# Attention inside a two-layer block: projections in the transposes' banks, a score bank per head, and the causal mask added by VectorE

## The reference

```
h = x_norm                                   # (2, 1024, 256)
q = (h @ wq) -> 32 heads of 64;  k, v = (h @ wk), (h @ wv) -> 8 heads of 64
scores = q @ k.T / sqrt(64)                  # each KV head serves 4 query heads
scores = where(causal, scores, min)
attn = softmax(scores);  out = (attn @ v) @ wo
```

## Time and profile before

| | us |
|---|---|
| median of 3 runs | 2073.08 |
| range of the runs | 2064.65 to 2074.55 |
| the profiled execution | 2076.18 |
| its span | 2074.5 |
| mean granted TensorE clock, share of full | 0.948 |
| PE busy | 1878.1 |
| DVE busy | 1062.9 |
| ACT busy | 899.0 |
| POOL busy | 234.4 |

### The profile page before, as it was taken

How to read it: one execution, slowest core, us unless ns; L and a number is a source line. 1 busy time by engine, 2 the same in 40 slices (tenths; PEclk the granted TensorE clock), 3 DMA queues, 4 the chain that set the end, 5 groups by cost and what they waited for, 6 DMA issues and landing times.

```text
span 2074.5 us, 32988 instructions
## 1 busy us (share of the span) xinstructions
PE 1878.1 (91%) x12734; PEld 1440.2 (69%) x12734; DVE 1062.9 (51%) x1977; ACT 899.0 (43%) x2028; POOL 234.4 (11%) x369
## 2 busy tenths in 40 slices
PE   6999699999999999999999999999934999999970
PEld 5666366766766766766766767767734999999970
DVE  4666466666666666666666666666630111111116
ACT  3444255555555555555555555555530122212210
POOL 2222100000000000000000000000023000000014
PEclk9999799999999999999999999999966999999995
DMA  2000210000000000000000000000025042012503
GB/s 77 0 0 0 100 41 8 1 1 8 1 1 9 1 1 9 1 1 9 1 1 9 1 1 1 1 1 1 1 89 188 26 144 83 25 53 67 196 30 109
DMA packets 44296, 67.25 MB, mean 32 GB/s; under 512 B 9952, under 2 KB 34528, under 8 KB 44192
## 3 DMA queue, kind: packets, MB, share of 16 engines
q1 hardware_dynamic: 35920, 45.11, 6.6%
q0 software_dynamic: 6208, 18.62, 2.7%
q10 hardware_dynamic: 2064, 2.10, 0.3%
HBM read 140.52 MB, written 16.52 MB: 76 GB/s over the span
## 4 chain that ended last, share of the span: by engine, by line
PE 71%; DVE 13%; ACT 7%; issue 5%; POOL 1%; DMA 1%; SPq 1%; DVEq 0%; another core or an unknown queue 0%; POOLq 0%; ACTq 0%
PE wide L1288 13%; PE bank L1208 13%; PE bank L1196 10%; PE wide L1176 7%; PE bank L1297 7%; PE wide L1180 6%; PE bank L1217 3%; ACT qhl L578 3%; DVE qhl L813 3%; PE wide L1152 3%; ACT arena L584 2%; DVE nmax L820 2%; PE wide L1026 2%; PE bank L1015 2%; PE wide L1179 1%
## 5 line engine op out<-in xcount | busy, mean ns | idle before, releaser
L820 DVE TENSOR_REDUCE nmax<-wide 128x1 f32<-128x896 f32 (+7 forms) x512 | 386.6, 755 | 217.5 <-PE wide L1180 207.2
L584 ACT ACTIVATE arena<-wide,nmax 128x896 f32<-128x896 f32 (+7 forms) x512 | 380.6, 744 | 265.4 <-DVE nmax L820 260.4
L1176 PE MATMUL wide<-khi,qhl 128*128 128x512 f32 (+3 forms) x768 | 351.7, 458 | 28.5 <-DVE vt L804 25.1
L1196 PE MATMUL bank<-ident,arena 128*128 128x128 f32 x2304 | 308.5, 273 | 0.0
L592 ACT COPY arena<-bank 128x512 f32<-128x512 f32 (+1 forms) x352 | 192.8, 548 | 253.4 <-PE bank L1196 241.5
L1180 PE MATMUL wide<-klo,qhl 128*128 128x512 f32 (+3 forms) x768 | 300.6, 396 | 0.0
L1208 PE MATMUL bank<-arena,vt 128*64 128x256 f32 x2304 | 295.2, 403 | 0.0
L1288 PEld LDWEIGHTS wide<-wo,arena 128*128 128x128 f32 x2496 | 287.1, 193 | 3.2 <-issue 1.3
L1288 PE MATMUL wide<-wo,arena 128*128 128x128 f32 x2496 | 287.5, 276 | 0.9 <-ACT wo L638 0.9
L1196 PEld LDWEIGHTS bank<-ident,arena 128*128 128x128 f32 x2304 | 261.8, 140 | 8.7 <-issue 0.4
L950 DVE TENSOR_TENSOR wo<-wide,wo 128x512 f32<-128x512 f32 x78 | 54.0, 692 | 415.1 <-PE wide L1288 415.1
(11 more groups left out here) (194 smaller groups left out, 1867.6 us busy)
## 6 DMA issues: line engine op xcount, KB each, us to landing
arena<-in_L_ffn_w SPq DMA_DIRECT2D x117, 1024.0 KB
wo<-xs SPq DMA_DIRECT2D x40, 128.0 KB, 2.0
xs<-zeros POOLq DMA_DIRECT2D x1, 4992.0 KB, 20.6
ys<-y_sb POOLq DMA_DIRECT2D x39, 128.0 KB, 2.0
x_all<-in_L_attn_x ACTq DMA_DIRECT2D x1, 2048.0 KB, 9.9
wq_g<-in_L_ffn_wq SPq DMA_DIRECT2D x8, 256.0 KB, 2.9
wo<-in_L_ffn_wo SPq DMA_DIRECT2D x16, 128.0 KB, 8.0
out<-x_all SPq DMA_DIRECT2D x16, 128.0 KB
```

What stands on the lines that cost most here:

```text
L584: nc.scalar.activation(probs[t % 2][:, h, 0:w], score_bank(h)[:, 0:w], ACT.Exp, bias=nmax[:, t % 2, h:h + 1], accum_out=rsum[:, t % 2, h:h ...
L820: nc.vector.tensor_reduce(nmax[:, t % 2, h:h + 1], score_bank(h)[:, 0:w], AX.X, ALU.max, negate=True).then_inc(S("nmax_ready"), 1)
L1176: mm(dst, q, khi[:, lo:lo + cols], start=True, stop=False)
L1196: ins = nc.tensor.transpose(turned[j % 3][:, h * P:(h + 1) * P], probs[t % 2][:, h, m * P:(m + 1) * P], ident[:])
```

## The change

Three things, all in the attention stage:

- One item per step (`STEP_ITEM`), at the end of the step, where item "b" stood. Items no longer use `wide`: items and transposed blocks take turns in one list, `TURNS`, over the same three banks. Each turn waits until the one three before it has been taken (`wait_bank`). V1 of the next pass is at step 7 of this one; the first pass's V1 is done ahead of step 0.
- In steps 0 to 3 each of the four heads has its own bank of `wide`. In steps 4 to 7 two heads share two banks each, as before. TensorE now waits for VectorE's maximum (`nmax_ready`, `scores_read`), no longer for exp.
- The mask matmul, `identb` and `above` are gone. VectorE adds a mask row block `causal` (1024 columns, f32, in SBUF; the last 128 hold the triangle) and takes the minimum of the negated sum in one `tensor_tensor_reduce`, which also writes the negated, masked scores into `probs`. ScalarE's exp reads them from there, with scale -1, in place. POOL fills `causal` once, ahead of the first `double`.

```
-PLACES = {(0, "a"): "V1", (0, "b"): "H0", (1, "a"): "H1", (1, "b"): "H2", (2, "a"): "F0", (2, "b"): "F1", (3, "a"): "F2", (3, "b"): "V2"}
+STEP_ITEM = ["H0", "H1", "H2", "V2", "F0", "F1", "F2", "V1"]
...
+FIRST_ITEMS = [(0, 0, 0), (0, 1, 0), (0, 2, 0), (0, "V", 0)]
+TURNS = FIRST_ITEMS + [x for t in range(TILES + 1)
+                       for x in ([(t - 1, m) for p in range(3) for m in third(t - 1, p)] if t else []) + ([item_of(t)] if t < TILES and item_of(t) else [])]
...
-        def score_bank(h):
+        def score_bank(t, h):
+            if t % TB < TB // 2:
+                return wide[:, h, :]
             return wide[:, 2 * (h % 2):2 * (h % 2) + 2, :].rearrange("p a b -> p (a b)")
...
+        causal = part(4 * G * SEQ + 8 * P, SEQ, "p (o c) -> p (o c)", o=1)
...
+            gp.wait_ge(S("rT_ready"), TB)
+            nc.gpsimd.memset(causal, 0.0).then_inc(S("causal_cleared"), 1)
+            gp.wait_ge(S("causal_cleared"), 1)
+            nc.gpsimd.affine_select(out=causal[:, SEQ - P:SEQ], in_=causal[:, SEQ - P:SEQ], compare_op=ALU.is_ge, fill=MASKED, base=0,
+                                    pattern=[[-1, P]], channel_multiplier=1).then_inc(S("causal_ready"), 1)
...
-                nc.scalar.activation(probs[t % 2][:, h, 0:w], score_bank(h)[:, 0:w], ACT.Exp, bias=nmax[:, t % 2, h:h + 1],
+                nc.scalar.activation(probs[t % 2][:, h, 0:w], probs[t % 2][:, h, 0:w], ACT.Exp, bias=nmax[:, t % 2, h:h + 1], scale=-1.0,
...
-                nc.vector.tensor_reduce(nmax[:, t % 2, h:h + 1], score_bank(h)[:, 0:w], AX.X, ALU.max, negate=True).then_inc(S("nmax_ready"), 1)
+                nc.vector.tensor_tensor_reduce(out=probs[t % 2][:, h, 0:w], in0=score_bank(t, h)[:, 0:w], in1=causal[:, SEQ - w:SEQ], scale=-1.0, scalar=-MASKED,
+                                               op0=ALU.add, op1=ALU.min, accum_out=nmax[:, t % 2, h:h + 1]).then_inc(S("nmax_ready"), 1)
...
+            def wait_bank(what):
+                if TURN_OF[what] >= 3:
+                    before = TURNS[TURN_OF[what] - 3]
+                    if len(before) == 3:
+                        wait_taken(before)
+                    else:
+                        pe.wait_ge(*evacuated(blocks_before(before[0]) + before[1]))
...
+            def scores_read(t, h):
+                ct = t % TB
+                if ct == 0:
+                    return G * (t - 1) + 3 + h // 2
+                if ct < TB // 2:
+                    return G * (t - 1) + h + 1
+                if ct == TB // 2 and h < 2:
+                    return G * (t - 1) + 2 * h + 2
+                return G * t + h - 1
...
-                    for item in [x for x in ITEMS if x == (n, "V", 1) or x == (n + 1, 2, 0)]:
-                        wait_taken(item)
-                if c >= 2:
-                    pe.wait_ge(S("exp_done"), c - 1)
+                if t:
+                    pe.wait_ge(S("nmax_ready"), scores_read(t, h))
...
-                    if half * HALF + cols == w:
-                        mm(dst[:, cols - P:cols], identb[:], above[:], start=False, stop=False)
```

More of the change, by code:

```diff
@@ L43, with item_of @@
 TILES = NSEQ * TB
-PLACES = {(0, "a"): "V1", (0, "b"): "H0", (1, "a"): "H1", (1, "b"): "H2", (2, "a"): "F0", (2, "b"): "F1", (3, "a"): "F2", (3, "b"): "V2"}
-def item_at(t, place):
+STEP_ITEM = ["H0", "H1", "H2", "V2", "F0", "F1", "F2", "V1"]
+def item_of(t):
     n, ct = divmod(t, TB)
[L52 to L60, removed]
+    kind, i = STEP_ITEM[ct]
+    if kind == "H":
+        item = n, int(i), 1
+    elif kind == "F":
+        item = n + 1, int(i), 0
+    else:
+        item = n + (i == "1"), "V", int(i) - 1
+    return item if item[0] < NSEQ else None
 def blocks_before(t):
@@ L221, in build, with bank_of @@
         pT = [[part(2 * G * SEQ + (i * TB + m) * G * P, G * P, "p (o c) -> p (o c)", o=1) for m in range(TB)] for i in range(2)]
-        turned = [bank[0], bank[1], bank[3]]
+        shared = [bank[0], bank[1], bank[3]]
+        def bank_of(what):
+            return shared[TURN_OF[what] % 3][:]
         rbc = [part(2 * G * SEQ + 2 * TB * G * P + i * 2 * P, 2 * P, "p (j c) -> p j c", j=2) for i in range(2)]
         spread = [part(2 * G * SEQ + 2 * TB * G * P + (2 + i) * 2 * P, 2 * P, "p (j c) -> p j c", j=2) for i in range(2)]
+        causal = part(4 * G * SEQ + 8 * P, SEQ, "p (o c) -> p (o c)", o=1)
         def turned_to(t, m):
-            src = turned[(blocks_before(t) + m) % 3]
+            src = bank_of((t, m))
             if m == t % TB + 1:
@@ L436, in _ @@
             for t in range(TILES + 1):
-                late, item = item_at(t - 1, "b") if t else None, item_at(t, "a")
-                if late and late[1] == 0:
+                item = item_of(t - 1) if t else None
+                if item and item[1] == 0:
                     if t > 1:
                         gp.wait_ge(S("rinv_spread"), t - 1)
-                    double(late[0], late[2])
+                    double(item[0], item[2])
                     doubled += 1
@@ L570, in evacuate @@
                 at = place_in_half(n, half)
-                src = item_bank(item)
+                src = bank_of(item)
                 act.wait_ge(S("projected"), n * 6 + half * 3 + i + 1)
@@ L592, in evacuate_part @@
                         nc.scalar.copy(*turned_to(t, m)).then_inc(S("pT_even"), 1)
-            nc.scalar.activation(junk[:, 0, 0:1], eps[:], ACT.Exp).then_inc(S("exp_loaded"), 1)
+            nc.scalar.activation(gmax[:, 0:1], eps[:], ACT.Exp).then_inc(S("exp_loaded"), 1)
             act.wait_ge(S("exp_loaded"), 1)
-            for i in range(3):
-                evacuate((0, i, 0))
+            for item in FIRST_ITEMS:
+                evacuate(item)
             for t in range(TILES + 2):
                 scored, turning = t < TILES, 1 <= t <= TILES
-                if t and item_at(t - 1, "b"):
-                    evacuate(item_at(t - 1, "b"))
+                if t and t <= TILES and item_of(t - 1):
+                    evacuate(item_of(t - 1))
                 if scored:
@@ L827, in evacuate_part @@
                         nc.vector.tensor_copy(*turned_to(t, m)).then_inc(S("pT_odd"), 1)
-            for i in range(3):
-                low_part((0, i, 0))
+            for item in FIRST_ITEMS:
+                low_part(item)
             for t in range(TILES + 2):
                 scored, turning, weighing = t < TILES, 1 <= t <= TILES, t >= 2
-                late = item_at(t - 1, "b") if t else None
-                if late and late[1] == "V":
-                    low_part(late)
+                item = item_of(t - 1) if turning else None
                 if scored:
                     maximum(t, 0)
-                if late and late[1] != "V":
-                    low_part(late)
+                if item:
+                    low_part(item)
                 if turning:
@@ L1130, in wait_taken @@
                     pe.wait_ge(S("qlo_ready"), 4 * n + 2 * half + i)
+            def wait_bank(what):
[3 more added lines that the diff above has]
+                        wait_taken(before)
+                    else:
+                        pe.wait_ge(*evacuated(blocks_before(before[0]) + before[1]))
             def project(item):
                 n, i, half = item
[L1134 to L1137, removed]
+                wait_bank(item)
+                to = bank_of(item)
                 if i == "V":
@@ L1184, in turn_part @@
                 for m in third(t, p):
-                    j = blocks_before(t) + m
-                    if j >= 3:
-                        pe.wait_ge(*evacuated(j - 3))
+                    wait_bank((t, m))
+                    to = bank_of((t, m))
                     if m == 0:
@@ L1218, in project_out @@
                 ins.then_inc(S("proj2"), 1)
-            for i in range(3):
-                project((0, i, 0))
+            for item in FIRST_ITEMS:
+                project(item)
             for t in range(TILES + 2):
@@ L1243, in _ @@
                     turn_part(t - 1, 2)
-                if item_at(t, "b"):
-                    project(item_at(t, "b"))
+                if scored and item_of(t):
+                    project(item_of(t))
             pe.wait_ge(S("acc_done"), BATCH * NKV * TB)
```

33 lines of the change are left out of this document (8 added, 25 removed).

## The result

The changed kernel takes 1997.70 us (median of 4 runs, 1996.32 to 1999.07) against 2073.61 us before, a ratio of 0.964 with a 95% interval of 0.962 to 0.967. The prediction was 1995 us. The profiled execution's span went from 2074.5 to 1997.4 us, 77.1 us less. The kernel before ran again beside each group of experiments, with medians of 2067.66 to 2074.36 us; one execution of it, of 3235.13 us at a mean granted clock of 0.55, is left out there.

A forecast was written before the change was run, and what follows sets the result against it. TensorE's rate of starting matmuls was taken as the bound. A pass: 78.5 - 3.3 - 1.8 - 1.7 + 1.75 + 0.1 = 73.5 us; all passes together save 78 us, giving a median of 1995 us, range 1965 to 2045.

The forecast's parts named there:

- The mask matmul: Removing it between khi and klo saves 3.3 us a pass, bounds 1.3 and 5.1 us.
- The pause: TensorE's wait in front of step 4 for VectorE's V2 copy goes: 1.65 us plus 0.15 us restart a pass.
- The half clock: Step 4's stretch at half clock goes with the wait before it: 1.7 us a pass, bounds 0 and 1.7 us.
- New waits: TensorE waits in step 2 (0.75 us), step 3 (0.7 us) and for item banks (0.3 us): 1.75 us a pass.
- VectorE's form: Fused add and minimum cost the same per column; accumulator 0.06 us a head, adding 0.1 us a pass.
- rival 1: VectorE's fused form runs at half rate and becomes the bound: 4.1 us a pass more than before, 2140 us, chance 0.12.
- ScalarE out of SBUF: Exp reading SBUF instead of PSUM differs by -0.07 to +0.07 us a head, which does not matter.
- POOL: Filling the mask constant before the first doubling, with three constants fewer, costs 0, at most 1 us.
- Scores wait for nothing: In steps 0 to 3, with a bank per head and release by VectorE, scores have no wait.
- Rivals 2 and 3: New waits lower TensorE's clock, 2030 us, chance 0.11; mask gives 0.04 us a head, banks stall every step, 2060 us, 0.07.
- The signs: Right: khi plus klo 0.34 to 0.45 us in step 2 or 3; wrong: TensorE waits in steps 5 to 7.
- The sum: A middle pass takes 71.7 + 1.75 + 0.1 = 73.5 us; first pass 4.5 us less, last 3.8 us less.

The follow-up runs named there:

- e1: Changed kernel with the 128-column mask matmul put back between khi and klo, beside VectorE's mask: 2043.56 us, 0.988 of the kernel before.
- e2: Changed kernel with the mask matmul put back at 16 columns instead of 128: 2045.45 us, 0.989 of the kernel before.
- e3: Changed kernel with score 0 of step 4 made to wait again for VectorE's copy of V2: 2016.53 us, 0.975 of the kernel before.
- e13: Kernel before, with VectorE copying V2 ahead of the last third's transposed block in step 3, not behind it: 2042.90 us, 0.985 of the kernel before.
- e9: Changed kernel with VectorE's low_part moved behind reciprocal and oT in step 2 alone: 1975.83 us, 0.956 of the kernel before.
- e10: As e9, with the items of steps 0, 6 and 7 projected behind the next step's score 0: 1966.07 us, 0.951 of the kernel before.
- e5: Changed kernel with TensorE's scores waiting for exp again instead of VectorE's maximum: 1996.66 us, 0.963 of the kernel before.
- e6: Changed kernel with two heads sharing each pair of banks in all steps, no bank per head: 1996.39 us, 0.963 of the kernel before.
- e11: As e3, with two unused VectorE additions of 256 columns ahead of V2's copy, lengthening the pause: 2027.57 us, 0.981 of the kernel before.

## Why the prediction was right, point by point

- **The mask matmul.** Predicted 3.3 us a pass. Matched intervals before and after, khi to the matmul behind klo, where another klo stands in front: 0.07 us a head at 128 columns and 0.13 at 256, 384 and 512, which is 3.6 us; put back by itself it costs 3.1, since some of it then falls into the wait for oT (0.67 us in the changed kernel, 0.28 in e1). The size held, the reading only in part: I had put it down to the mask's columns plus the reload of q's weights that a short matmul can't cover. e2 shows that fewer columns save nothing, and the weight loads' rows bear out the uncovered reload.
- **The pause.** Predicted 1.8 us; gone, as the windows of step 3 show. Its reverse (e3) costs 1.3 us, since in the new order VectorE has less to do in front of V2's copy: 6.4 us of work in e3's step 3 where it had 8.1.
- **The half clock.** Predicted 1.7 us, found 1.6 (e13) and absent from the middle passes after. The step "the half clock follows on that pause" is true of what the kernel before does in 15 passes of 16, the last having no pause; as a rule it failed: pauses of 1.3 to 1.9 us put back did not bring it back in most passes, nor did 1.82 us in e13's first pass. The number was right because the change took the pause away altogether, which left nothing for the rule to decide.
- **New waits.** Predicted 0.75 us for oT in step 2, measured 0.67. For step 3 I had predicted 0.7 us; there is next to no wait (the window shows TensorE busy throughout), but the step's own work was 0.6 us more than my sum of pieces, so 6.51 us stand against 6.6. The banks of the items were priced at 0.3 us; the intervals between the last transposes and the items of steps 0, 6 and 7 show 0.3, 0.2 and 0.2 us, 0.7 in all. e9 gave 0.9 us back and e10 another 0.84, together 1.7 us against the 1.75. That the sum fits so well is luck: one term was 0.7 us too high, one 0.4 too low.
- **VectorE's form.** Full rate, as the two-input row said: rival 1 is refuted by the 1.224 us row. The accumulator's read, 0.083 us, lay near the 0.06 taken. The Trainium skill's statement that an accumulator output makes two instructions (VectorE: DVE Perf Modes, Two Vector instructions with no wait between them) agrees with the trace, where 308 reads of 0.083 us stand beside the fused forms. The Trainium skill's rule on halved throughput (Vector Engine (DVE) Microarchitecture Reference, Points that are easy to get wrong) is for two SBUF sources. The one operation of that kind here, L958 in the mixture of experts, which has no accumulator output, takes 0.48 us for 256 columns; at twice the 1.05 ns a column of the reduce the columns alone would take 0.54 us, an estimate, so this trace doesn't bear the rule out for it.
- **ScalarE out of SBUF.** +0.03 us a head, inside the bounds and hidden.
- **POOL.** No price to be seen: the first score starts at 254.6 us instead of 254.0, and at 253.9 to 256.1 in the experiments.
- **Scores wait for nothing.** In the trace no score matmul of the middle passes waits for a maximum; e5 and e6 fit that.
- **Rivals 2 and 3.** The wait of step 2 did not lower the clock in the middle passes: all eight windows read 1.00. In the first pass it fell in step 2, behind a wait of 1.92 us for a transfer. The shared banks stall for 0.7 us a pass, not in every step, and the mask gave 0.13 us a head, not 0.04.
- **The signs.** Two of them were set badly. From khi to the transpose behind klo it is 0.44 us in step 2, inside the 0.34 to 0.45 given, but 0.57 in step 3. And TensorE does wait in steps 6 and 7, for the items' banks, which was listed as a sign of being wrong although 0.3 us were charged for it.
- **The sum.** 73.5 us a pass was predicted and 73.44 measured. The terms found, 3.6 + 1.65 + 1.6 less 1.7 to 1.8 of new waits, give 5.1 of the 5.0 us. Part of the fit is luck: the predicted work of the eight steps adds up to 72.0 us, not to the 71.7 used, and single steps are off by up to 0.6 us both ways. The first pass gave 3.3 us instead of 4.5, because of the half clock in its step 2: e5 and e6, which have none there, take 66.4 us for it. The last gave 4.5 instead of 3.8.

## What to carry to other kernels

Where TensorE issues without a gap, count what stands between two matmuls: a narrow one adds its own weight load and leaves the load of the next one uncovered, however few columns it has, and moving its work to an engine with slack buys that back, but only if this engine is not the one that TensorE waits for a moment later. Look at each pause of TensorE for what follows it: a copy of 0.42 us, moved ahead of one of 0.68 in another engine's order, shortened the pause by 0.6 us a pass and was worth 2.2. And test the parts by themselves: the two that sound like the idea (a bank per head, the early release) did nothing when taken back one at a time, and a move that helps in one step can cost as much in others.

## What the runs showed of the hardware that was not expected

- A mask matmul of 16 columns costs as much as one of 128: 0.70 us from khi to the next transpose with either, 0.57 without. The load of the same q weights is made again for klo in either case (0.19 us), 0.23 us ahead of klo without the mask and 0.03 us ahead with it.
- The granted clock fell to half behind a 1.65 us pause in the middle passes of the kernel before, and stayed at 1.00 behind pauses of 1.3 and 1.5 us, and mostly of 1.9 us, at the same place of the changed kernel. With the same work and the same pause it fell in two of e11's 14 middle passes and not in the others.
